# Spreading the edge sort over the counting steps and sorting one group late on TensorE, in a four-layer graph network on one core

## The reference

```
x = layernorm(x + gin(x, edges))                  # sums of neighbours, two small MLPs
x = layernorm(x + relational_attention(x, ...))   # per edge scores, softmax per source node
x = layernorm(x + gat_with_gru(x, ...))           # per edge scores, softmax per destination
x = layernorm(x + chebyshev(x, ...))              # four layers of two hops on the same graph
```

## Time and profile before

| | us |
|---|---|
| median of 3 executions | 5783.12 (5781.89 to 5783.99) |
| the profiled execution, its own time | 5754.43 |
| its span | 5752.0 |
| stretch of the loop in the trace | 232 to 1237 |
| busy in the whole span: TensorE, VectorE, ScalarE, GpSimdE | 3741.0, 3246.9, 2402.4, 1999.9 |

### The profile page before, as it was taken

One profiled execution on the slowest core, in us unless ns is written; L12 is line 12 of the kernel. 1 busy time (PEld: TensorE's weight loads), 2 busy tenths in 40 slices (PEclk: granted clock), 3 DMA queues, 4 the chain that ended last, 5 costly groups with the idle time before them and its releaser, 6 DMA issues. The chain is left out here.

```text
span 5752.0 us, 85345 instructions
## 1 busy us (share of the span) xinstructions
PE 3741.0 (65%) x22841; PEld 2853.2 (50%) x22842; DVE 3246.9 (56%) x10027; ACT 2402.4 (42%) x6907; POOL 1999.9 (35%) x2011
## 2 busy tenths in 40 slices
PE   3377777759208677667840777777784078777987
PEld 0133444438107666666730766666674067654443
DVE  8777777742207555555730655555575888744444
ACT  0244444433107445445730544444463755523321
POOL 5000000033362666666127166666620056502210
PEclk9999999979556555555555555555555555578997
DMA  0000000020110111111011011111102000000000
GB/s 9 6 0 0 0 0 0 0 111 1 30 35 12 33 34 34 33 34 33 12 25 40 8 34 34 34 34 33 34 16 110 0 1 1 1 9 3 4 1 13
DMA packets 72029, 122.17 MB, mean 21 GB/s; under 512 B 40834, under 2 KB 45867, under 8 KB 71147
## 3 DMA queue, kind: packets, MB, share of 16 engines
q0 software_dynamic: 50048, 77.77, 5.3%
q1 hardware_dynamic: 20972, 24.30, 1.4%
q10 hardware_dynamic: 640, 15.65, 0.6%
HBM read 97.94 MB, written 19.68 MB: 20 GB/s over the span
## 5 line engine op out<-in xcount | busy, mean ns | idle before, releaser
L943 POOL DMA_INDIRECT adjacency<-dram_table,sorted_dst x1564 | 1508.3, 964 | 1379.6 <-issue 393.6
L954 PE MATMUL bank<-adjacency 128*128 x3520 | 828.6, 408 | 106.1 <-issue 106.1
L954 PEld LDWEIGHTS bank<-adjacency 128*128 128x128 f32 x3520 | 763.2, 316 | 167.9 <-issue 167.0
L1049 DVE TENSOR_REDUCE adjacency<-bank 128x1 f32<-128x128 f32 x440 | 128.3, 292 | 1176.4 <-remote 1086.3
L988 PE MATMUL bank<-adjacency 128*128 x5280 | 305.2, 191 | 490.9 <-issue 480.7
L1017 ACT ACTIVATE adjacency<-adjacency 128x128 f32<-128x128 bf16 x1760 | 572.1, 399 | 2.4 <-DVE adjacency L1102 2.2
L988 PEld LDWEIGHTS bank<-adjacency 128*128 128x128 bf16 x5280 | 278.6, 111 | 492.5 <-issue 465.4
L526 ACT ACTIVATE adjacency<-bank 128x400 f32 x590 | 297.5, 504 | 491.0 <-PE bank L501 354.9
L1640 PE MATMUL bank<-adjacency,cheb_parts 128*128 128x512 f16 (+1 forms) x2100 | 437.4, 367 | 52.2 <-ACTq L95 31.4
L1010 ACT ACTIVATE adjacency<-bank 128x512 bf16<-128x512 f32 x220 | 129.8, 590 | 793.7 <-remote 680.9
L966 PE MATMUL bank<-ident_b,adjacency 128*128 128x128 bf16 x1760 | 268.5, 302 | 279.0 <-DVE adjacency L1073 141.2
(11 more groups left out here) (446 smaller groups left out, 8116.6 us busy)
## 6 DMA issues: line engine op xcount, KB each, us to landing
adjacency<-dram_table,sorted_dst POOLq DMA_INDIRECT x1564
dram_adjacency<-adjacency ACTq DMA_DIRECT2D x1, 15200.0 KB, 38.0
adjacency<-dram_adjacency SPq DMA_DIRECT2D x1, 15200.0 KB, 40.0
dram_table<-adjacency SPq DMA_DIRECT2D x2, 1212.5 KB, 10.5
dram_nodes<-x_nodes SPq DMA_DIRECT2D x1, 800.0 KB, 3.3
x_nodes<-dram_nodes SPq DMA_DIRECT2D x1, 800.0 KB, 4.2
x_nodes<-in_x SPq DMA_DIRECT2D x1, 768.0 KB
out_nodes<-x_nodes SPq DMA_DIRECT2D x1, 768.0 KB
```

Of the source, the lines that this page charges most:

```text
L943: pool.indirect_dma_start(ring[:, j % (RG * TG), :], None, dram["table"], bass.IndirectOffsetOnAxis(ap=S.dst_i[:, j:j + 1], axis=0)).then_ ...
L954: ins = pe.matmul(sums[i % 2][:, 0:W1], reach[:, i % WRING, t, :], ring[:, bass.ds(at_r[i], TG), :][:, t, 0:W1], start=(t == 0), stop=(t = ...
```

## The change

VectorE's work for a group is cut in three (`dve_group`): the one-hot of tiles stands behind the first step of the three, lanes and rows behind the second, the product with the values behind the third. Each has its own wait: `part_read` for the buffer of the tiles, `lanes_read` for those of rows and lane values, `group_hot` for the product.

TensorE runs one group later: the row matmuls of the group before stand behind the first step (`pe_rows`), the tile matmuls of that same group for the first value behind the second step and for the second value behind the third (`pe_tiles`). Before, the tile matmuls were those of the group before and the row matmuls those of the current one; now both are of the group before. The first wait of `pe_tiles` is for ScalarE's copy made in the same three steps, and for the tiles' one-hot. ScalarE's copy (`act_part`) stands in the first step, between L526 and L517. `tile_of` gets a first column of -1, so that the one-hot of tiles is made a group late as well. After the loop come the row matmuls, the copy and the tile matmuls of the last group. The set-up clears row_hot and lane_value instead of tile_hot and part. The instructions of a group are the same in number and size.

```diff
-                dve.wait_ge(group_read.sem, g + 1)
-                dve.tensor_tensor(lane_hot[:, b], ...).then_inc(group_hot.sem, 1)
-                dve.tensor_tensor(row_hot[:, b], ...)
-                dve.tensor_scalar(tile_hot[0:ROWS, b, :], ...)
-                dve.wait_ge(group_hot.sem, g + 1)
-                dve.tensor_tensor(lane_value[:, b], ...).then_inc(group_valued.sem, 1)
+            if n >= EACH:
+                dve_group(dve, turn, i // EACH, i % EACH)
...
+    def dve_tiles(dve, turn, g):
+        dve.wait_ge(part_read.sem, g + 1)
+        dve.tensor_scalar(tile_hot[0:ROWS, 1 - g % 2, :], ...).then_inc(tiles_made.sem, 1)
+    def dve_group(dve, turn, g, part_of):
+        if part_of == 0:
+            dve_tiles(dve, turn, g)
+        elif part_of == 1:
+            dve.wait_ge(lanes_read.sem, g + 1)
+            dve.tensor_tensor(lane_hot[:, b], ...).then_inc(group_hot.sem, 1)
+            dve.tensor_tensor(row_hot[:, b], ...)
+        else:
+            dve.wait_ge(group_hot.sem, g + 1)
+            dve.tensor_tensor(lane_value[:, b], ...).then_inc(group_valued.sem, 1)
...
+    def pe_rows(pe, g):
+        pe.wait_ge(group_valued.sem, g + 1)
+        for t in range(TG):
+            ins = pe.matmul(part_v[0:ROWS, :], row_hot[:, 1 - g % 2, :, t], lane_value[:, 1 - g % 2, :, :, t], ...)
+        ins.then_inc(part_made.sem, 1)
+    def pe_tiles(pe, g, v, read, last=False):
+        b = 1 - g % 2
+        lanes = part[0:ROWS, b, v * P:(v + 1) * P]
+        if v == 0:
+            pe.wait_ge(part_copied.sem, g + 1)
+            pe.wait_ge(tiles_made.sem, g + 1)
+        ins = pe.matmul(left_v[:, v * LEFT:(v + 1) * LEFT], lanes, tile_hot[0:ROWS, b, 768:NT], ...)
+        if v == 0:
+            ins.then_inc(lanes_read.sem, 1)
+        pe.matmul(low_v[v][:, :], lanes, tile_hot[0:ROWS, b, 0:512], ...)
+        ins = pe.matmul(high_v[:, v * 256:(v + 1) * 256], lanes, tile_hot[0:ROWS, b, 512:768], ...)
+        if v == 1:
+            ins.then_inc(read.sem, 1)
...
-            if i % EACH == EACH - 1:
+            if n >= EACH:
                 g = i // EACH
-                pe.wait_ge(group_valued.sem, g + 1)
-                pe.wait_ge(part_copied.sem, g + 1)
-                for t in range(TG):
-                    pe.matmul(part_v[0:ROWS, :], row_hot[:, b, :, t], lane_value[:, b, :, :, t], start=(t == 0), stop=(t == TG - 1))
-                pe_part(pe, b, group_read)
+                if i % EACH == 0:
+                    pe_rows(pe, g)
+                else:
+                    pe_tiles(pe, g, i % EACH - 1, part_read)
...
             act.activation(A4[...], psum[i % RING][...], ACT.Copy).then_inc(copied.sem, 1)
+            if n >= EACH and i % EACH == 0:
+                act_part(act, i // EACH)
             act_cell(act, next_g[i], next_j[i], (i + AHEAD_R) % CELLS)
-            if i % EACH == EACH - 1:
-                act.wait_ge(part_made.sem, g + 1)
-                act.activation(part[0:ROWS, g % 2, :], part_v[0:ROWS, :], ACT.Copy).then_inc(part_copied.sem, 1)
```

More of the change, by code:

```diff
@@ L288, in on_dve @@
         V(dve.scalar_tensor_tensor(near, fifth, -float(SLOTS), near, ALU.mult, ALU.add))
-        V(dve.tensor_tensor(S.tile_of[rows, :], at, near, ALU.add))
+        dve.memset(S.tile_of[rows, 0:1], -1.0)
+        V(dve.tensor_tensor(S.tile_of[rows, 1:NG + 1], at, near, ALU.add))
     def on_pe(pe):
@@ L443, in build_adjacency @@
     done, copied = k.sig("cells_done"), k.sig("cells_copied")
-    group_hot, group_valued, group_read = k.sig("group_hot"), k.sig("group_valued"), k.sig("group_read")
+    group_hot, group_valued, part_read = k.sig("group_hot"), k.sig("group_valued"), k.sig("part_read")
     part_made, part_copied, set_up, iota_made = k.sig("part_made"), k.sig("part_copied"), k.sig("sort_set_up"), k.sig("tiles_iota")
-    sort_done = k.sig("sort_done")
+    sort_done, lanes_read, tiles_made = k.sig("sort_done"), k.sig("lanes_read"), k.sig("tiles_made")
     rounds = ASTEPS // TURN
@@ L475, in dve_turn @@
         if n >= EACH:
-            dve.sem_inc(group_read.sem, -(n // EACH))
+            dve.sem_inc(lanes_read.sem, -(n // EACH))
+            dve.sem_inc(part_read.sem, -(n // EACH))
             dve.sem_inc(group_hot.sem, -(n // EACH))
[L479 to L483, removed]
-        ins.then_inc(part_made.sem, 1)
[L485 to L489, removed]
+    def dve_tiles(dve, turn, g):
+        dve.wait_ge(part_read.sem, g + 1)
+        dve.tensor_scalar(tile_hot[0:ROWS, 1 - g % 2, :], iota_t[0:ROWS, :], S.tile_of[0:ROWS, bass.ds(turn * (TURN // EACH) + g, 1)], None,
+                          ALU.is_equal).then_inc(tiles_made.sem, 1)
@@ new lines, in pe_rows @@
+    def pe_rows(pe, g):
+        pe.wait_ge(group_valued.sem, g + 1)
+        for t in range(TG):
+            ins = pe.matmul(part_v[0:ROWS, :], row_hot[:, 1 - g % 2, :, t], lane_value[:, 1 - g % 2, :, :, t], start=(t == 0), stop=(t == TG - 1))
+        ins.then_inc(part_made.sem, 1)
+    def pe_tiles(pe, g, v, read, last=False):
[4 more added lines that the diff above has]
+            pe.wait_ge(tiles_made.sem, g + 1)
+        ins = pe.matmul(left_v[:, v * LEFT:(v + 1) * LEFT], lanes, tile_hot[0:ROWS, b, 768:NT], start=False, stop=last and v == 1)
+        if v == 0:
+            ins.then_inc(lanes_read.sem, 1)
+        pe.matmul(low_v[v][:, :], lanes, tile_hot[0:ROWS, b, 0:512], start=False, stop=last)
+        ins = pe.matmul(high_v[:, v * 256:(v + 1) * 256], lanes, tile_hot[0:ROWS, b, 512:768], start=False, stop=last and v == 1)
+        if v == 1:
+            ins.then_inc(read.sem, 1)
@@ L543, in on_dve @@
         dve.memset(nought[:, :], 0.0)
-        dve.memset(tile_hot[:, 1, :], 0.0)
-        dve.memset(part[:, 1, :], 0.0)
+        dve.memset(row_hot[:, 1], 0.0)
+        dve.memset(lane_value[:, 1], 0.0)
         dve.drain().then_inc(set_up.sem, 1)
@@ L548, in on_dve @@
         dve.sem_inc(hot_read.sem, RING)
-        dve.sem_inc(group_read.sem, 1)
+        dve.sem_inc(lanes_read.sem, 1)
+        dve.sem_inc(part_read.sem, 2)
         with dve.Fori(0, rounds) as turn:
@@ L562, in on_pe @@
         pe_turn(pe, rounds, ASTEPS - rounds * TURN)
-        pe.wait_ge(part_copied.sem, 1)
-        pe_part(pe, NG % 2, sort_done, True)
+        pe_rows(pe, 0)
+        for v in range(2):
+            pe_tiles(pe, 0, v, sort_done, True)
     def on_act(act):
```

29 lines of the change are left out of this document (15 added, 14 removed).

## The result

The changed kernel takes 5621.8 us in the median of 4 executions (5618.0 to 5624.3), against 5783.6 (5781.9 to 5787.3) for the kernel before beside it: a ratio of 0.9719 with a 95% interval of 0.9702 to 0.9736, or 161.8 us less. The forecast was 5618.4, in a range of 5598 to 5685. On another chip the same kernel was 164.4 us faster (5590.8 against 5755.2).

A forecast was written before the change was run, and what follows sets the result against it. A ring from L501 over ScalarE's store back to L501, 1.11 us a step, was taken as bound; 49 rounds at 20.47 - 17.07 save 166.6 us, less 1.9 once, so 5783.1 - 164.7 = 5618.4, range 5598 to 5685.

The forecast's parts named there:

- the ring: In each step L501 waits for ScalarE's store of the step before, so a step costs 1.11 us.
- VectorE's waits: Waits for buffers and one-hots at VectorE's new places in a group: forecast to cost nothing.
- The group: Three steps of the loop: 1.42, 1.13 and 1.11 us, in all 3.66 (bounds 3.64 and 3.96), where it was 4.36.
- the hand-off: Second step: tile matmuls wait for ScalarE's copy, done at 1.71, and start at 1.85 on the scale of T(0).
- The head: Start of a round, T(11) to T(1), with ScalarE's register reads: 4.63 us (bounds 4.4 and 5.21), where it was 5.21.
- T(11): T(i) is the start of L501 in step i of a round; T(11) is that of the last step.
- TensorE's head: TensorE's own cost at the start of a round, taken as 0.36 us: T(11) to T(0) was 2.50, not 2.14.
- The slow stretch: 3.3 us at 1.2 GHz after a round's start: 0.35 us per round taken, between 0 and 1.0, against 1.05 before.
- Once-only costs: Outside the rounds: +1.6 us for the last group's chain after the loop, +0.3 for the set-up, together +1.9.
- VectorE as bound: Rival: VectorE sets the pace at 4.2 to 4.6 us per group, 5665 to 5743; chance 0.10, shared with ScalarE's hand-off.
- the low clock for most of the loop: Rival: clock falls to 1.2 GHz between the heads, round 21.55 us, 5838, so slower; chance 0.04.
- no change: Rival: a hidden wait keeps the group's work behind the third step, round near 20.4 us, 5780; chance 0.03.

The follow-up runs named there:

- the filling matmuls: Changed kernel plus six zero-adding matmuls of 512 columns behind each round's last step: 194.4 us under the kernel before, mean round 16.51 us.
- the last kernel: Changed kernel with TensorE's sort work cut evenly, twelve zero-adding matmuls, two row reads on ScalarE, rounds of 24 steps: 256.8 us under the kernel before, ratio 0.9557.

## Why the prediction was right

**The mechanism** was right, and both halves were tested: the ring L501, ScalarE's store, L501 set the pace, and what earns is that TensorE's sort work lies in the ring's free time. VectorE's waits cost next to nothing, as forecast, and its new places earn 2 to 3 us.

**The group.** Forecast 1.42, 1.13 and 1.11; measured 1.43, 1.11 and 1.11. The one miss is the hand-off: L507 starts 0.29 us after L525, not 0.43, mostly because the wait after ScalarE's end was 0.05 us and not the 0.14 seen before L501.

**The head.** Forecast 4.63 from T(11) to T(1), measured 4.46, toward the lower bound of 4.4. The rule of the Trainium skill weighed there (Perfetto Trace Analysis, Per-engine timelines), by which a sequencer goes on past a waiting instruction, would have kept 5.21; on this point the trace went the other way. ScalarE idled 2.67 us at its reads also where the instruction ahead of them had moved. The head is 0.73 of the 3.48 us that a round became shorter; no run moved ScalarE's copy alone, so that its new place is what shortened the head is argued from the two traces, and what it says of the sequencer stays open.

**TensorE's head** was wrong, without harm. The step "the second 0.36 is what the head costs TensorE itself" took what was left over, beside 0.72 + 0.90 us of queued matmuls, for the whole. TensorE's head takes 2.2 us from T(11), before the change and after it. So the idle time that was forecast as 1.97 us ahead of T(1) came as 1.5 ahead of T(0) and 0.3 ahead of T(1). TensorE's head stayed hidden under ScalarE's here, and came out as soon as that one was cut.

**The slow stretch** was the least certain term. Forecast 0.35 per round as a third of 1.0; measured 0.51 (the means after a head are 1.22, 1.46 and 1.16 against 1.11 each), with a full price of 0.7 to 0.9 in two rounds of three. That the idle time at the head is its cause was only argued then; the filling matmuls, which change nothing else, show it for the changed kernel, where the clock then stays at 1.00. The Trainium skill (TensorE: Matmul & The Clock Gate, HAM oscillation) describes a loop whose every turn starts at the low clock, behind waits for a DMA that are longer than the gaps here; in this case a gap of 2.0 us went with the stretch in every round, and one of 1.5 us in two rounds of three. Why the third escapes, with the same gap, stays open.

**The sum.** A round at full clock was forecast at 16.72 and is 16.51 (the kernel with filling matmuls); with the slow stretch 17.07 against 17.03. So the close agreement owes something to two misses of 0.2 us with opposite signs. Once-only costs were forecast at 1.9 and are 2.7, most of it in the chain after the last step (2.26 for 1.6). 49 rounds at 20.47 - 17.07 gave 166.6; the loop gave 169.2, and the executions 161.8 and 164.4.

**The rivals.** VectorE as bound, the low clock for most of the loop and "no change" did not come. The first of them had the right sum for a group: VectorE's 3.61 us is the bound late in the rounds of the last kernel, where a group otherwise takes 3.35. The 0.63 us that it counted for VectorE's head was a wait for the ring; the idle time that VectorE has at a head without a wait is 0.41 us on average in the changed kernel (19.6 us in 48 times).

## What to carry to other kernels

Where a dependent chain over two engines sets the pace, count the free time of each engine per link of that chain, and cut any block that is longer than it: TensorE at 75% busy was no bound, but 1.6 us of work in one place was. A long wait on an engine says little by itself; ask who waits for that engine in turn. At the head of a hardware loop, queue work on an engine ahead of its register reads: the reads then run below it. On TensorE even matmuls that add zeros paid here, by keeping the clock; look at the granted clock to see in how many rounds they do.

## What was not expected of the hardware

- TensorE's head of a round takes 2.2 us from its last L525 for 12 registers, 3.0 for 24, and 2.2 and 2.8 in turn for 6, while matmuls already queued go on; 1.3 us of added matmuls in that time cost nothing and made the loop of the changed kernel 25 us shorter.
- Idle gaps of 1.5 and 0.3 us in a round of 17 us, with TensorE busy for 89% of the loop, stood ahead of a granted clock of 0.51 for 3.3 us in two rounds of three; with matmuls in the first gap the clock stayed at 1.00. In the kernel before with the same matmuls, one gap of 1.1 us stood ahead of the stretch in some rounds and of none in others.
- ScalarE's reads cost 0.059 us per register between 28 and 52 registers, but 18 registers in rounds of 6 took 2.6 and 4.3 us in turn.
